# Second message passing over 440 block-sorted edge tiles, sums kept in SBUF

## The reference

```python
edge_dst, edge_src = (edge_index[0], edge_index[1])   # receiver = src, sender = dst
pd0 = p0[edge_dst]
ip1 = jnp.einsum('eum,eum->eu', p1[edge_dst], p1[edge_src]) / 3.0
s0 = jnp.concatenate([pd0, pd0, ip1], axis=-1)
w = ssp(edge_attr @ W_f1) @ W_f2 * (ssp(s0 @ W_s1) @ W_s2)
w1, w2, w3, w4 = jnp.split(w, 4, axis=-1)
x0e, x1e = split_irreps(x[edge_src])
out0 = w1 * x0e * sh0[:, None] + w4 * (jnp.einsum('eum,em->eu', x1e, sh1) / jnp.sqrt(3.0))
out1 = w2[:, :, None] * x0e[:, :, None] * sh1[:, None, :] + w3[:, :, None] * x1e * sh0[:, None, None]
edge_feat = merge_irreps(out0, out1)
out = jax.ops.segment_sum(edge_feat, edge_dst, num_segments=old_x.shape[0])
```

## Time and profile before

| | us |
|---|---|
| median of three runs | 6303.36 (6297.29 to 6304.94) |
| the profiled execution | 6299.19 |
| its span in the trace | 6297.4 |
| mean granted clock of PE | 0.857 |
| PE busy in the span | 4863.1 |
| DVE busy | 3717.9 |
| POOL busy | 3133.7 |
| ACT busy | 2080.9 |

### The profile page before, as it was taken

The page is one execution under the profiler, slowest core; times in us unless marked ns, Lnnn a source line. Parts: engine busy times, 40 slices in busy tenths (PEclk is TensorE's granted clock), DMA queues, the critical chain, the costliest instruction groups (busy, mean ns, idle before and its releaser), DMA issues. The chain is left out here.

```text
span 6297.4 us, 79602 instructions
## 1 busy us (share of the span) xinstructions
PE 4863.1 (77%) x17537; PEld 2615.2 (42%) x17538; DVE 3717.9 (59%) x9258; ACT 2080.9 (33%) x4483; POOL 3133.7 (50%) x2844
## 2 busy tenths in 40 slices
PE   5545388777776888897784798888888888888797
PEld 2222155422223444454553565333334343343373
DVE  7311144477777777734235212877877787777654
ACT  1000011122222333211222102666666666666511
POOL 0677600066665666510223202777777777877500
PEclk9777588888888899898896899998888898888898
DMA  3101200055555555503534313888888888888833
GB/s 127 47 31 43 76 27 27 25 170 172 172 170 144 167 167 169 165 27 120 179 124 138 119 44 99 201 191 193 194 193 190 195 195 191 195 190 192 186 120 133
DMA packets 359491, 867.04 MB, mean 138 GB/s; under 512 B 86738, under 2 KB 109889, under 8 KB 358998
## 3 DMA queue, kind: packets, MB, share of 16 engines
q0 software_dynamic: 212464, 648.95, 42.2%
q1 hardware_dynamic: 127615, 174.83, 8.4%
q10 hardware_dynamic: 19190, 41.03, 1.7%
HBM read 643.81 MB, written 221.22 MB: 137 GB/s over the span
## 5 line engine op out<-in xcount | busy, mean ns | idle before, releaser
L766 POOL DMA_INDIRECT s_krow<-mid_att_rows,s_ix x440 | 420.4, 956 | 738.7 <-ACT s_ix L802 496.7
L1990 POOL DMA_INDIRECT mid_acc<-m_out,m_il x416 | 711.3, 1710 | 138.4 <-issue 114.5
L1977 POOL DMA_INDIRECT m_drow<-mid_drow,m_ig x416 | 457.7, 1100 | 477.7 <-DMA m_ig<-in_dst_ix 281.4
L2200 PE MATMUL m_pws<-m_w,m_hid 32*128 32x512 f32 x832 | 516.2, 703 | 202.8 <-DVE m_hid L2031 161.2
L992 PE MATMUL m_pm<-m_vrow,m_same 128*128 128x512 f32 x880 | 546.5, 710 | 150.3 <-DVE m_vrow L935 138.1
L2208 PE MATMUL m_pm<-m_msg,m_same 128*128 128x512 f32 x832 | 547.9, 745 | 133.5 <-issue 74.8
L840 PE MATMUL s_pq<-queries_q,s_same 128*128 x880 | 493.8, 699 | 110.4 <-issue 69.7
L919 POOL DMA_INDIRECT m_vrow<-mid_att_rows,m_ix x440 | 460.0, 1045 | 234.3 <-issue 127.1
L2201 PE MATMUL m_pwf<-m_w,m_hid 32*128 32x512 f32 x832 | 524.8, 713 | 0.0
L2171 PEld LDWEIGHTS m_pip<-keep_ident,m_drow 128*128 128x128 f32 x2496 | 412.9, 226 | 260.7 <-issue 254.1
L442 POOL DMA_INDIRECT mid_slots<-f_rec_now,f_row_now x416 | 419.1, 1007 | 160.8 <-issue 139.1
(11 more groups left out here) (389 smaller groups left out, 9419.4 us busy)
## 6 DMA issues: line engine op xcount, KB each, us to landing
mid_att_rows<-f_rows SPq DMA_DIRECT2D x75, 256.0 KB
mid_ys<-e_y SPq DMA_DIRECT2D x57, 256.0 KB
mid_acc<-e_zero ACTq DMA_DIRECT2D x26, 512.0 KB
g_q<-mid_qT SPq DMA_DIRECT2D x50, 256.0 KB, 4.2
g_a<-mid_acc SPq DMA_DIRECT2D x50, 256.0 KB, 3.1
mid_srow<-t_srow SPq DMA_DIRECT2D x5, 2240.0 KB
keep_w<-in_w SPq DMA_DIRECT2D x16, 512.0 KB
s_krow<-mid_att_rows,s_ix POOLq DMA_INDIRECT x440
```

What stands on the lines that cost most here:

```text
L766: pool.indirect_dma_start(krow[:, k % SS, :], None, io["att_rows"][1], bass.IndirectOffsetOnAxis(ap=ix[:, k:k + 1], axis=0),).then_inc(s_g ...
L1977: pool.indirect_dma_start(row, None, table, bass.IndirectOffsetOnAxis(ap=ig[:, k // EH, n, k % EH:k % EH + 1], axis=0),).then_inc(s_g[k % ...
L1990: pool.indirect_dma_start(io["acc1"][k % NACC], bass.IndirectOffsetOnAxis(ap=il[:, k // EH, k % EH:k % EH + 1], axis=0), out[:, k % R, :], ...
L2200: pe.matmul(pws[k % 2][:], hid[0:HID, par, cols], w_2[0:HID, :], start=True, stop=True)
```

## The change

- A second sort, by `src`, runs among tiles 10 to 19 of the tables in `front0`, with the steps of the first and in its buffers, and leaves `row1` (the place of each edge) and `owner1` (the block of each of 440 tiles). The loops over table tiles of PE and DVE are written out. The counting, its lines, its last pass and `leads1` are gone. SP lays 22 transfers of 400 KB with empty records into `slots1` between the mixer's weights and the first `f_xin`.
- The host lays `dst`, `src`, the four `sh` and the 32 attributes of an edge together as a record of 39 words (156 bytes). `put_chunk` loads eight columns of them and scatters them with eight indirect transfers of 128 records. There are 16 such chunks in `merge0`, 7 in `gates0`, 12 in `tables1` and 17 in `mixer1`, 416 scatters in all, all on POOL.
- `mixer1` also copies `keep.X` to `x_kept` in DRAM, and DVE then clears it, since `keep.acc` is the same SBUF. `merge1` reads `x_kept` back.
- `edges1` does 440 tiles. Indices, `sh` and attributes come from the loaded records; PE turns the attributes, ACT copies them. The equality matrix is made from SBUF by three DVE instructions. The message has one DVE instruction of 256 columns in place of two of 128, and no last addition: PE adds that part in a second pair of passes. The scatter with addition is replaced by a POOL addition in SBUF.
- `clear_sums`, its zero tile and both DRAM accumulators are gone.

```diff
+def put_chunk(pool, io, keep, rec, s_rec, s_put, first, i, count):
+    def load(j):
+        need(pool, s_put[j % 3], 16 * PUT * (j // 3))
+        cols = slice(PUT * (first + j), PUT * (first + j + 1))
+        pool.dma_start(rec[:, j % 3], io["edge_rec"][:, cols, :]).then_inc(s_rec[j % 3], 16)
...
+    for k in range(PUT):
+        col = PUT * (first + i) + k
+        pool.indirect_dma_start(
+            io["slots1"], bass.IndirectOffsetOnAxis(ap=keep.row1[:, col:col + 1], axis=0), rec[:, i % 3, k, :], None,
+        ).then_inc(s_put[i % 3], 16)
...
 (front0, SP)
+                empty = io["slots1"].rearrange("(p t) k -> p t k", p=P)
+                for b in range(SN):
+                    sp.dma_start(empty[:, SB * b:SB * (b + 1), :], io["empty1"][:, :, :]).then_inc(s_empty1, 16)
...
 (front0, DVE tables)
-                        if isinstance(n, int) and n < 2 * U:
-                            order(n)
+                        if n < 2 * U:
+                            order(n, by_receiver)
+                        elif n < 4 * U:
+                            if n == 2 * U:
+                                vec.wait_ge(s_k, STEPS)
+                            order(n - 2 * U, by_sender)
...
 (front0, DVE mix)
-                    for k in range(EU):
-                        if k == 6 and not last_pass(b):
-                            mix_sums(b)
-                        if k == 12 and not last_pass(b):
-                            mix_values(b)
-                            mix_elu(b, last)
-                        count(b, k)
+                    mix_sums(b)
+                    mix_values(b)
+                    mix_elu(b, last_tile(b))
...
 (merge0, POOL)
+                for i in range(PUT0):
+                    put_chunk(pool, io, keep, rec, s_rec, s_put, 0, i, PUT0)
+                all_put(pool, s_put, PUT0)
...
 (experts0, ACT)
-                act.wait_ge(s_zero, 1)
-                cleared = clear_sums(act, s_z, zero, io["acc1"], D)
...
 (mixer1, DVE)
+                vec.wait_ge(s_park, 16 * NB)
+                vec.memset(keep.acc[:], 0.0)
...
 (edges1, POOL)
-                    pool.indirect_dma_start(
-                        io["acc1"][k % NACC], bass.IndirectOffsetOnAxis(ap=il[:, k // EH, k % EH:k % EH + 1], axis=0),
-                        out[:, k % R, :], None, compute_op=ALU.add,
-                    ).then_inc(s_add[k % R], 16)
+                    pool.wait_ge(s_row, t + 1)
+                    need(pool, s_add, t)
+                    pool.tensor_tensor(keep.acc[:, node, :], keep.acc[:, node, :], out[:, k % R, :], ALU.add).then_inc(s_add, 1)
...
 (edges1, PE)
-                    pe.matmul(pm[:], same[:, k // B % 2, k % B, :], msg[:, k % 2, :], start=True, stop=True).then_inc(s_seg, 1)
+                    pe.matmul(pm[:], mine, msg[:, k % 2, P:P + D], start=True, stop=False)
+                    pe.matmul(pm[:, 0:P], mine, msg[:, k % 2, 0:P], start=False, stop=True).then_inc(s_seg, 1)
```

More of the change, by code:

```diff
@@ L704, in _ @@
                 mix(NT // 2, 0)
-                mix(NT // 2, 1)
+                sums(NT - 1, True)
                 pe.wait_ge(s_loc, 1)
@@ L1940, in at, with steps, bodies @@
+        s_go2 = s.sem("go_scalar")
+        DV = 5
         def at(b, k):
-            if isinstance(b, int) and not 0 <= EU * b + k < ET:
+            if isinstance(b, int) and not 0 <= EU * b + k < ST:
                 return None
             return b + k // EU, k % EU
+        def steps(b):
+            return range(ST - EU * b) if isinstance(b, int) and b == EP - 1 else range(EU)
+        def bodies(eng, body):
+            body(0)
+            with eng.Fori(1, EP - 2) as b:
+                body(b)
+            body(EP - 2)
+            body(EP - 1)
@@ new lines, in add, with owners @@
+                    pool.tensor_tensor(keep.acc[:, node, :], keep.acc[:, node, :], out[:, k % R, :], ALU.add).then_inc(s_add, 1)
+                def owners(b, k):
+                    _, four = nc.values_load_multi_w_load_instructions(
+                        keep.owner1[0:1, bass.ds(EU * b + k, LAG)], engines=[mybir.EngineType.Pool], min_val=0, max_val=NT - 1,
+                        skip_runtime_bounds_check_because="each owner counts the starts of 25 blocks that a tile has reached, less one, and the first starts at 0")
+                    return four
@@ L1995, in body @@
                 def body(b):
-                    for k in range(EU):
+                    for k in steps(b):
                         if there := at(b, k + GATHER):
                             gather(*there)
-                        if there := at(b, k - 3):
-                            scatter(*there)
+                        if at(b, k - LAG):
+                            if k % LAG == 0:
+                                node = owners(b, k)
+                            add(EU * b + k - LAG, k, node[k % LAG])
@@ L2001, in _ @@
                 for k in range(GATHER):
                     gather(0, k)
-                passes(pool, EB, body)
-                scatter(EB - 1, EU - 3)
-                scatter(EB - 1, EU - 2)
-                scatter(EB - 1, EU - 1)
-                for r in range(R):
-                    pool.wait_ge(s_add[r], 16 * (ET // R))
+                bodies(pool, body)
+                node = owners(0, ST)
+                for k in range(LAG):
+                    add(ST - LAG + k, k, node[k])
             @block.vector
@@ L2586, in program @@
                 run(front0)
-                run(leads1)
                 run(scores0)
@@ L2706 @@
     "xn": [NP, D],
+    "x_kept": [NP, D],
     "ys": [XS * P, D],
```

463 lines of the change are left out of this document (200 added, 263 removed).

## The result

The changed kernel takes 6711.73 us (median of four runs, 6709.65 to 6719.36) against 6300.32 (6275.12 to 6304.94) for the kernel before: a ratio of 1.066, 95% interval 1.063 to 1.069. It is 411 us slower where 90 less were forecast, and lies outside the range.

A forecast was written before the change was run, and what follows sets the result against it. POOL's list was taken to bound `edges1`, a third of the span, and PE `merge0` and `mixer1`. Terms -106 - 20 + 25 + 20 - 30 + 11 + 13 - 3 = -90 gave 6209 us from 6299.19; range 6070 to 6370.

The forecast's parts named there:

- Cost 0, with PE as cover: Record scatters in `merge0`, `gates0`, `tables1` and `mixer1`: POOL's list fits inside each stage, so they add 0 us.
- the rival: The scatters slow the four stages they move into: 0.65 us lost for each of 416, +272, 6481 us; chance 0.20.
- I take 4.65, and 4.70 with coupling.: `edges1`: us a tile with DVE and POOL partly excluding one another; 440 tiles give 2088 us, +13.
- the 3.62 of the prediction: `edges1`: DVE's own list of instructions after the change, 3.62 us a tile.
- The second rival: `edges1`: exclusion costs all, DVE and POOL each waiting whole instructions, 5.05 us a tile, 6363 us; chance 0.13.
- `front0`: Constants, `front0` and `leads1` together: counting leaves, a second sort and empty records come; forecast difference -82 us.
- 15.4: `mix` in `front0`: a regular pass falls from 20.0 to 15.4 us without counting; -106 us over 23 passes.
- the 25 taken: Second sort in tiles 10 to 19 of `front0`: mostly covered, +25 us (0 to 60).
- `experts0`: ACT's copy `e_xT` no longer comes 32.62 us late behind 26 clearing transfers: -30 us.
- the clearing: End of `mixer1`: DVE clears 12800 columns when PE is done, +11 us.
- `merge1`: `merge1` and the constants together: -3 us; the stage table has -2 for `merge1` and on.
- the prediction's signs of being wrong: `merge0`, `tables1` or `mixer1` growing over 20 us, PE issue waits there, or an `edges1` pitch outside 4.5 to 4.9.

The follow-up runs named there:

- e12: Changed kernel with DVE adding from PSUM in `edges1` and POOL clears behind scatters (256 columns; 128 in `gates0`): 6214.59 us, ratio 0.985 to the kernel before.
- e4: Changed kernel with DVE adding each tile's sums from PSUM in `edges1`, POOL only gathering, ACT not copying out: `edges1` takes 2082 us.
- e5: Changed kernel with POOL's addition in `edges1` replaced by two clears of 512 columns (sums lost): `edges1` takes 1949 us.
- e16: The changed kernel again, unedited, in a set without a crawl: 5912.97 us against 5748.81 for the kernel before, ratio 1.028.
- e9: Kernel before with only the table loops of DVE and PE in `front0` written out: 5687.91 us (one run), ratio 0.987 to the kernel before.
- e15: e12 with POOL's list in `front0` written out and the clear ahead of each scatter there: 5680.23 us against 5748.81 for the kernel before, ratio 0.988.
- e8: Kernel before with three POOL clears of 16 columns behind each 8-byte scatter of `front0`: 5888.90 us against 5762.83, ratio 1.022.

## Why the prediction was wrong

**The step that failed first: "Cost 0, with PE as cover"**, for the scatters in four stages. POOL's own list was near (the 128 scatters of `merge0` take 170 us from the first to the last), and hiding was asked of the wrong thing. Dense indirect transfers keep PE from issuing and make its signals, on which DVE and ACT wait, late, by 54 and 56 us in the two shown. The cost is 145 + 53 + 4 + 162 = 364 us, 0.87 each for 416; the rival said 0.65 and had 0.20. `tables1` cost 4 us. Its scatters come in eights, 1.27 us apart as elsewhere, with POOL's additions between the eights, so that 96 of them take 179 us, 1.87 us each in the mean. That fits both the pitch that e12 found free and the delay with which the crawl sets in, but was not tried by itself. The evidence was in the trace before: the earlier trace rows show PE with half its pace in the stretch of the earlier trace rows, and I priced it as a rival rather than a term, because `scores0` seemed immune. It was not, it seems: 685 us before, 563 to 566 in the sets that do not crawl.

**The second: "I take 4.65, and 4.70 with coupling."** The stage took 2338 us, (2338 - 20)/440 = 5.27 us a tile. Against e4, DVE's instructions are longer by 3 x 123 + 87 + 356 + 111 + 62 ns and a quarter of 832 for the tag, 1.2 us a tile (the 111 and 62 from groups not shown, 400 against 289 and 485 against 423). By its busy time DVE works 2187/440 = 4.97 us a tile, which is the 3.62 of the prediction and the whole of POOL's addition, 1.35 here. So nothing to speak of was hidden under `m_w`. That is the rule of the Trainium skill as the prediction quoted it ("SBUF — State Buffer", sections "Who interferes with whom" and "Summary: rules for kernel authors": the second to issue fully blocks), with no overlap at all. What failed behind it is the coupling: DVE is idle for the other 0.30 us, where 0.05 was allowed, and what it is short of there stays open. e5 agrees with what the first of these sections says of the other case, that a POOL instruction which only writes does not hold up one with two SBUF inputs. The second rival (5.05, chance 0.13) was nearest in its number, but not in that both engines wait whole instructions: POOL's addition is 1.35 us in the mean where it was 1.26.

**Wrong in its parts: `front0`.** -184 with the constants in place of -82. The first product of `mix` comes at 586 us and not 677, 92 earlier where some 45 later were forecast; the tables end at 541 us and not 664, in spite of the second sort. From there to `scores0` it is 487 us in place of 579, 93 less where 126 were forecast. A regular pass of `mix` takes 12.2 us, not 15.4: by the window above PE is busy all the time at a granted clock of 0.99 where it had 0.85, its 32 products of the first kind take 3.7 us a pass and not 6.1 (67.2/18 and 134.6/22, groups not shown), and I had kept the old pace in the products. But seven passes now stand beside the scatters and take 255 us, where two did and took 107. Why the crawl hurt the tables less after than before was not found, and some of it is chance: with the same code in `front0` the tables end between 452 and 564 us in the runs of the two sets that crawl, and the stage takes 1013 to 1079. In the sets without a crawl the second sort costs 43 us (e16 443, e9 400, both loops written out), above the 25 taken, and `scores0` starts at 830 us in e16 against 925 in e9, 95 earlier.

**Right:** `experts0` -32 (-30), the clearing +13 (+11), `merge1` -2. The shares: +145 + 53 + 4 + 175 + 257 - 184 - 32 - 2 - 3 = +413, the difference of the spans. Three of the prediction's signs of being wrong came: `merge0` and `mixer1` grew by over 20 us, PE shows issue waits there, and the pitch of `edges1` is above 4.9.

The best version measured in a calm set is e15: nothing crawls there, and its addition is DVE's. Its `edges1`, with 24 tiles more, takes 2049 us, against 2013 in e9 with as few loads of instructions, and one more sort and POOL's longer list in `front0` are paid on top.

## What to carry to other kernels

Work put on an idle engine is only free if the path that it shares is idle too: look in the trace for "issue" waits of other engines in the stretches where that kind of instruction already runs, and price them as a term. Leave a pause between indirect transfers that POOL issues in rows (here 1.46 us from start to start was enough and 1.27 was not), as long as POOL's list stays shorter than the stage, and put no wait for the clear directly ahead of the transfer. Give an addition whose input lies in PSUM to DVE; on POOL it needs a copy to SBUF, and here its whole time was added to DVE's list as well. And give the kernel before each side edit of the new one, such as written-out loops, before you put a per cent down to the idea.

## What the hardware showed unexpectedly

- Beside indirect transfers 1.26 us apart, PE made 40 passes in 100 us of `merge0` (87 with a clear of one column between them), at 1.46 us 417, without any 432; in `mixer1` 210 at 1.35 us and 519 at 1.46. Scatters of 156 bytes and gathers act alike, at a DMA share of 0.13 to 0.19.
- In the crawl two of PE's semaphore updates came 54 and 56 us behind the products that they report, in place of 0.014.
- This comes and goes between sets of runs: 6300 or 5750 us for the same kernel before, on one chip both (6338 and 5747).
- POOL's clears, which only write, do hold up DVE's cast of 4 columns and the instruction ahead of it: 732 and 533 ns in e5, 170 and 208 in e4.
- A wait for a POOL clear, with an increment, between that clear and an indirect transfer costs 0.6 us (gap 0.79 against 0.17).
- The same `edges1` takes 2088 us in e8 with 129 loads of instructions and 2013 in e9 with 14.
